# Column differences moved behind the last tile's second norm, and the first loads of down's weights moved behind the load for the fifth matrix

## The chip, the cores and the metric

The kernel runs on the 8 cores of one Trainium2 chip. Each core computes 1,024 of the 8,192 rows of the result: cores 2b and 2b+1 take the upper and the lower half of batch b. The cores share no data while they run. The time of a run is the device time of the slowest core, in microseconds (us).

## The reference, cut to what matters

The input x has shape (4, 2048, 2048). One layer of linear attention over the columns is followed by a gated feed-forward, each with a norm ahead of it and one behind it.

```python
X = Z_in[:, :256, :]; Y = Z_in[:, 256:, :]
att = relu((B_l @ X).T @ (C_l @ X))          # att[-1, -1] = 0
attn = concat(X + A_l @ (X @ att), Y + r_l * (Y @ att))

x = x + layernorm(attn(layernorm(x)))
# ffn(x), INTER = 5632, HIDDEN = 2048
g = (x @ gate_w.T) * gate_s
u = (x @ up_w.T) * up_s
out = ((silu(g) * u) @ down_w.T) * down_s
x = x + layernorm(ffn(layernorm(x)))
```

## The kernel before, in words

Everything is recorded in one list per engine (`Prog`), in the order of the calls in the source. An engine works its list strictly in that order, and a wait at the head of it holds everything behind it. GpSimd (POOL) has one list that holds nearly all loads of weights; SyncE (SP) has the loads and stores of x. POOL's DMAs also convert float32 in memory to bf16 on the core.

**First stage, attention and the two norms.** The 1,024 rows of a core are 8 tiles of 128, worked in the order `ORD` (index `i`, tile `dt = ORD[i]`; for `i` of 4 and more the two are the same). Tile `i` passes through `t0` (products with the attention matrix, L443), the first norm (`norm_a_...`, `x1`, L508, which also stores the tile by `spill[i]`), then the second norm: `square2` (ACT, L518: sum of squares into `q2a`), `norm_b_dv` (DVE, L525 to L531: three tiny operations, the last of which needs `q2a`), `norm_b_ac` (ACT L538 and L540, one tiny DVE operation L542, and ACT L545, which writes the normed tile `lc`). `ltr(i)` (L555) transposes `lc` on TensorE through two banks; ACT copies one out (L340), DVE the other (L341), both to `bop`. For tiles 4 to 7, three DVE subtractions (L570) then make the tile's columns of `T1`, `T2` and `T4`, operands of the second stage. They read both of the tile's copies.

**Second stage, gate and up.** The weights come as 44 packed matrices `m` (even: gate, odd: up; two of 5632/128 blocks each), 1 MB each on the core. `load_w(m)` puts matrix `m` into one of three buffers (`m % 3`). Matrices 0 and 1 are multiplied plainly (`plain_pe`, L732), first for the rows of half `h = 0` and then for `h = 1`. The matrices from 2 on go through seven products of 8 matmuls each in place of eight (Strassen-Winograd, `product(m, k)`, L799), for which `combos(m)` forms four sums of the matrix's quarters on DVE (L759). The loop over `m` issues products (m,6), (m,5), (m,7), (m+1,1), (m,4), (m+1,2), (m,3), and then `load_w(m + 3)`, which waits for product (m,3) to free the buffer. The first sum for matrix m+1 is recorded right behind product (m,6).

**Third stage, down, in blocks.** `down` (L837) multiplies the gated blocks `hdn` with down's weights `dwb`, of which `load_dw(gi)` loads block `gi` (0.5 MB on the core) into one of six buffers. The first `down` is recorded at m = 5, behind product (5,5). From then on it is woven into the loop over `m`.

**The stretch between the stages** is what the change touches. While tile 7 passes its norms, TensorE works plain products of the half h = 0, which need tiles 0 to 3 only: (0,0) and (1,0), then `ltr(6)`, then (0,1) and (1,1). Next comes `ltr(7)`, products (2,1) and (2,2), the four plain products of the half h = 1 (64 matmuls), and the loop. POOL's list there is: `load_w(2)`, the six `load_dw(0..5)`, `load_w(3)` (waits for `w_free[0]`, the last plain product with matrix 0), `load_w(4)` (waits for `w_free[1]`, the last one with matrix 1), `load_w(5)` (product (2,3)), `load_w(6)` (product (3,3)). `load_dw(gi)` waits for the stored and normed tile `i = 5 + gi // 2`, whose x buffer it overwrites.

Of the kernel before, what the change touches and what calls it, by code (L numbers as in the profile page):

```python
# [12 lines left out]
ALU = mybir.AluOpType  # L13
AX = mybir.AxisListType

P = 128
D = 2048
R = 1024
DT = R // P
# [9 lines left out]
ORD = [2, 3, 0, 1, 4, 5, 6, 7]  # L29
# [5 lines left out]
DS = 6  # L35
# [6 lines left out]
B11, B21, B12, B22, T1, T2, T4 = range(7)  # L42
# [69 lines left out]
def build_nc():  # L112
# [14 lines left out]
    pg = Prog(nc, es)  # L127
# [82 lines left out]
    def bank16(b):  # L210
        return ps[:, b, :].bitcast(BF16)
# [17 lines left out]
    x_ld, spill, lnf_done, x1_tok = {}, {}, {}, {}  # L229
# [108 lines left out]
    def evict(eng, out, in_, after):  # L338
        if eng == "scalar":
            return pg.ac(lambda e: e.copy(out, in_), after)  # L340
        return pg.dv(lambda e: e.tensor_copy(out, in_), after)  # L341
# [120 lines left out]
    sq1_t, va_t, ra_t, sqb_t, ltr_t, lnfT_t = {}, {}, {}, {}, {}, {}  # L462
    bop_t = {}
# [58 lines left out]
    def norm_b_dv(i):  # L522
        dt = ORD[i]
        c = slice(dt, dt + 1)
        a = pg.dv(lambda e: e.scalar_tensor_tensor(  # L525
            vb[:, c], s2a[:, c], -1.0 / (D * D), s2a[:, c],
            ALU.mult, ALU.mult), [x1_tok[i]])
        cn_t[i] = pg.dv(lambda e: e.scalar_tensor_tensor(
            cN[:, c], m1s[:, c], -1.0 / D, rN[:, c], ALU.mult, ALU.mult),
            [ra_t[i]])  # L530
        sqb_t[i] = pg.dv(lambda e: e.scalar_tensor_tensor(  # L531
            vb[:, c], q2a[:, c], 1.0 / D, vb[:, c], ALU.mult, ALU.add),
            [a, sqb_t[i]])

    def norm_b_ac(i):
        dt, sl = ORD[i], xslot[i]
        c = slice(dt, dt + 1)
        a = pg.ac(lambda e: e.activation(  # L538
            lnB[:, c], vb[:, c], AF.Ln, bias=eps_c[:, :]), [sqb_t[i]])
        a = pg.ac(lambda e: e.activation(  # L540
            r2[:, c], lnB[:, c], AF.Exp, scale=-0.5), [a])
        b = pg.dv(lambda e: e.scalar_tensor_tensor(  # L542
            ng2[:, c], s2a[:, c], -1.0 / D, r2[:, c], ALU.mult, ALU.mult),
            [a])
        lnf_done[i] = pg.ac(lambda e: e.activation(  # L545
            lc[:, i % 2, :], xr[:, sl, :], AF.Identity, scale=r2[:, c],
            bias=ng2[:, c]), [b])

    def ltr(i):
        dt = ORD[i]  # L550
        for g in range(2):
            bk = LNB[g]
            for k in range(8):
                ht = g * 8 + k
                t = pg.pe(lambda e, bk=bk, k=k, ht=ht: e.transpose(  # L555
                    bank16(bk)[:, k * P:(k + 1) * P],
                    lc[:, i % 2, ht * P:(ht + 1) * P], idm[:, 0, :]),
                    [lnf_done[i], *tok_bank[bk]] if k == 0 else (),
                    sig=(k == 7))
            o = (dt % 4) * P  # L560
            ev = evict(("scalar", "vector")[g],
                       bop[:, (B11, B21, B12, B22)[g + 2 * (dt // 4)], :,
                           o:o + P],
                       bank16(bk).rearrange("p (k c) -> p k c", c=P), [t])
            tok_bank[bk] = (ev,)
            lnfT_t.setdefault(dt // 4, {})[g] = ev
        if dt >= 4:
            for out, in0, in1 in ((T1, B12, B11), (T2, B22, T1), (T4, B21, T2)):
                bop_t[out] = pg.dv(lambda e, out=out, in0=in0, in1=in1:
                                   e.tensor_tensor(  # L570
                    bop[:, out, :, o:o + P], bop[:, in0, :, o:o + P],
                    bop[:, in1, :, o:o + P], ALU.subtract),
                    [*lnfT_t[0].values(), *lnfT_t[1].values(),
                     bop_t.get(in1)])
        ltr_t[i] = t


    w_ld, dw_ld, w_free = {}, {}, {}

    def load_w(m, after=()):  # L580

        s = m % WS
        w_ld[m] = pg.dma("gpsimd", f"w{s}", wr[:, s, 0:4, :],
                         t_gu.ap()[m], after)

    def dw_at(gi):
        return {IT - 2: dwx0, IT - 1: dwx1}.get(gi, dwb[:, gi % DS, :])

    def load_dw(gi, after=()):
        dw_ld[gi] = pg.dma("gpsimd", f"d{gi % DS}", dw_at(gi)[:, :],  # L590
                           t_dw.ap()[gi * P:(gi + 1) * P, :], after)
# [78 lines left out]
    for i in range(2, DT):  # L670
# [15 lines left out]
        t0(i, 0)  # L686
        t0(i, 1)
        ltr(i - 2)
        if nxt:
            prep_cast(i + 1, 0)  # L690
# [51 lines left out]
    def plain_post(m, gi, h, bk, t):  # L742
        f = gated if m else silu_of
        tok_bank[bk] = (f(gi, h, 2 + gi, ps[:, bk, :], [t]),)
# [46 lines left out]
    def product(m, k):  # L791
        a_bk = RING[2 * (m - 2) % 3]
        b_bk = RING[(2 * (m - 2) + 1) % 3]
        bk = {2: CB, 5: b_bk, 3: b_bk}.get(k, a_bk)
        ws, bs = PROD[k]
        need = [w_ld[m], *tok_bank[bk], cmb.get((m, ws)), bop_t.get(bs),
                *(lnfT_t[bs // 2].values() if bs < T1 and k != 7 else ())]
        for c in range(8):
            t = pg.pe(lambda e, c=c: e.matmul(  # L799
                ps[:, bk, :], wr[:, m % WS, ws, c * P:(c + 1) * P],  # L800
                bop[:, bs, c, :], start=(k in (1, 2, 5) and c == 0),
                stop=(c == 7), skip_group_check=(k not in (1, 2))),
                need if c == 0 else (), sig=(c == 7))
        if k == 1:
            copied(m, "P1", bk, t)
        elif k == 2:
            joined_up(m, "P1", bk, t, 0, 0)
        elif k == 6:
            copied(m, "U2", bk, t)
        elif k == 5:  # L810
            st[(m, "P5")] = t
            tok_bank[bk] = (t,)
        elif k == 7:
            copied(m, "U3", bk, t)
            joined_up(m, "U3", b_bk, st[(m, "P5")], 1, 1)
        elif k == 4:
            tok_bank[bk] = (used(m, 1, 0, ps[:, bk, :], t),)
        else:
            joined_up(m, "U2", bk, t, 0, 1)
            w_free[m] = t  # L820
# [49 lines left out]
    last = DT - 1  # L870
# [4 lines left out]
    x1(last)  # L875
    square2(last)
    ltr(last - 1)
    g1, u1 = plain_pe(0, 1, 0, 2), plain_pe(1, 1, 0, 3)
    norm_b_dv(last)
    norm_b_ac(last)  # L880
    plain_post(0, 0, 0, 0, g0)
    plain_post(1, 0, 0, 1, u0)
    plain_post(0, 1, 0, 2, g1)
    plain_post(1, 1, 0, 3, u1)
    ltr(last)
    tmp_free[0] = tmp_free[1] = (ltr_t[6],)
    tmp_free[2] = tmp_free[3] = (ltr_t[7],)
    product(2, 1)
    product(2, 2)
    for gi in range(DS):  # L890
        i = 5 + gi // 2
        load_dw(gi, [spill[i], lnf_done[i]])
    for n, (m, gi) in enumerate(((0, 0), (0, 1), (1, 0), (1, 1))):
        t = plain_pe(m, gi, 1, n)
        plain_post(m, gi, 1, n, t)
# [5 lines left out]
        bop[:, T3, :, :], bop[:, B22, :, :], bop[:, B12, :, :], ALU.subtract),  # L901
        [w_free[1], *lnfT_t[1].values()])
    load_w(4, [w_free[1]])

    for m in range(2, NM):
        b = next(k for k in range(NB) if 2 * (m // 2) < BASE[k] + BLKS[k])
# [26 lines left out]
        if b > 0 and n == 3:  # L933
            for li in range(BLKS[b - 1]):
                gi = BASE[b - 1] + li + DS
# [247 lines left out]
```

How the kernel before makes its waits and increments, by code:

```python
                def body(eng, ename=ename):  # L91
                    seen = {}
                    for after, fn, sem, n in self.lists[ename]:
                        for tok in after:
                            if tok is None:
                                continue
                            s, v = tok
                            if v > seen.get(s, 0):
                                eng.wait_ge(self.sems[s], v)
                                seen[s] = v
                        if fn is None:
                            continue
                        ins = fn(eng)
                        if sem is not None:
                            ins.then_inc(self.sems[sem], n)
```

## Time and profile before

| | |
|---|---|
| runs of the kernel (us) | 1055.66, 1155.41, 1055.39; median 1055.66 |
| profiled execution (us) | 1055.02 |
| its slowest core, core 7, from first to last instruction | 1053.5 |
| spans of cores 0 to 7 | 1050.1, 1052.8, 1052.2, 1050.6, 1049.5, 1051.4, 1050.7, 1053.5 |
| TensorE busy on core 7 | 1006.6 us, 96% of the span |
| VectorE busy | 591.6 us, 56% |
| ScalarE busy | 289.5 us, 27% |
| chain that ended last, by engine | PE 81%, DMA 5%, DVE 5%, ACT 5% |

The second run is a disturbed one, in which the whole chip is slower; it is left aside. Times in the rows are counted from the span's start. A row of the timeline is: start, length, engine, line, operation, what it writes and reads, count; the bracket behind it is the time that the engine sat idle before it, and what ended that. PE is TensorE, PEld its weight load, DVE VectorE, ACT ScalarE, POOL GpSimd. L86 is the helper that records every DMA.

### The profile page before, as it was taken

The page shows a single profiled execution, that of the slowest core. Times are in us where ns is not written, and L with a number is a line of the kernel's source. Part 1 is how long each engine was busy: PE and PEld are TensorE (multiplying, and loading weights), DVE is VectorE, ACT ScalarE, POOL GpSimd, SP SyncE. Part 2 cuts the span into 40 slices and gives each one's busy share as a digit, 9 for nine tenths or more (in the row PEclk, how much of TensorE's full clock was granted, in tenths as well). Part 3 has the DMA queues.
Part 4 walks back from the last instruction along what each step waited for, and adds up shares of the span by engine and source line. Part 5 has one row for each costly group of instructions (what it writes and reads, how often), then busy time and mean ns, then how long its engine had stood idle before and what let it go on. Part 6 is the DMA issues. An engine that isn't in the chain of part 4 may idle for free.

```text
span 1053.5 us, 12922 instructions; the slowest of 8 cores (1049.5 to 1053.5 us)
## 1 busy us (share of the span) xinstructions
PE 1006.6 (96%) x4868; PEld 461.8 (44%) x4868; DVE 591.6 (56%) x814; ACT 289.5 (27%) x427; POOL 52.1 (5%) x98
## 2 busy tenths in 40 slices
PE   2899999999999999999999999999999999999993
PEld 0345554444444444444444444444444444444441
DVE  3656667445646555654655555654555555555577
ACT  3555666622112012111112112111112121112266
POOL 0000000100001001001001001010010010001010
PEclk9999999999999999999999999999999999999997
DMA  7602331794234625626527329229238247338479
GB/s 210 144 1 110 113 138 50 149 162 81 46 69 79 116 52 87 114 41 104 97 40 123 77 40 147 54 40 159 41 53 147 40 73 128 49 71 162 119 120 200
DMA packets 18636, 101.35 MB, mean 96 GB/s; under 512 B 2192, under 2 KB 2320, under 8 KB 9744
## 3 DMA queue, kind: packets, MB, share of 16 engines
q0 software_dynamic: 13536, 75.50, 42.0%
q1 hardware_dynamic: 4608, 24.38, 6.5%
q10 hardware_dynamic: 432, 0.64, 0.3%
q8 instruction: 40, 0.66, 0.3%
q14 instruction: 20, 0.16, 0.1%
HBM read 152.95 MB, written 16.78 MB: 161 GB/s over the span
## 4 chain that ended last, share of the span: by engine, by line
PE 81%; DMA 5%; DVE 5%; ACT 5%; issue 3%; POOL 0%; DVEq 0%; ACTq 0%; SPq 0%; POOLq 0%
PE ps L799 45%; PE ps L837 28%; PE ps L443 4%; DMA dwb<-dw 3%; PE ps L412 2%; DMA wr<-gu 1%; DVE xr L508 1%; ACT lc L545 1%; DMA xr<-xtop 1%; ACT lc L468 1%; ACT pc L334 1%; PE ps L732 1%; ACT bop L340 1%; DVE acc L826 0%; DVE att L426 0%
## 5 line engine op out<-in xcount | busy, mean ns | idle before, releaser
L799 PE MATMUL ps<-bop,wr 128*128 128x512 bf16 x2352 | 520.0, 379 | 1.7 <-DMA wr<-gu 1.7
L799 PEld LDWEIGHTS ps<-bop,wr 128*128 128x128 bf16 x2352 | 229.9, 98 | 279.3 <-issue 2.5
L837 PE MATMUL ps<-dwb,hdn 128*128 128x512 bf16 x1344 | 307.2, 379 | 1.0 <-DMA dwb<-dw 0.9
L852 DVE TENSOR_TENSOR acc<-acc,ps 128x2048 f32<-128x2048 f32 x70 | 160.2, 2288 | 213.2 <-PE ps L837 213.2
L837 PEld LDWEIGHTS ps<-dwb,hdn 128*128 128x128 bf16 x1344 | 131.3, 98 | 160.5 <-issue 2.9
L772 ACT COPY tmp<-ps 128x512 f32<-128x512 f32 x126 | 73.3, 582 | 347.7 <-PE ps L799 347.7
L780 DVE TENSOR_TENSOR tmp<-tmp,ps 128x512 f32<-128x512 f32 x126 | 86.5, 686 | 92.1 <-ACT tmp L772 46.0
L759 DVE TENSOR_TENSOR wr<-wr 128x1024 bf16<-128x1024 bf16 x168 | 114.2, 686 | 8.2 <-DMA wr<-gu 3.7
L443 PE MATMUL ps<-att,xT 128*128 128x512 bf16 x512 | 117.4, 379 | 0.5 <-DVE xT L341 0.5
L710 ACT ACTIVATE sg<-tmp,cpks 128x512 bf16<-128x512 f32 x63 | 45.5, 722 | 239.7 <-DVE tmp L780 239.7
L443 PEld LDWEIGHTS ps<-att,xT 128*128 128x128 bf16 x512 | 49.5, 98 | 58.2 <-issue 1.0
L86 POOL DMA_DIRECT2D wr<-gu x44 | 23.5, 534 | 888.9 <-PE ps L799 625.6
L721 DVE SCALAR_TENSOR_TENSOR hdn<-tmp,cpks,sg 128x512 bf16<-128x512 f32 x63 | 47.3, 751 | 6.6
L412 PE MATMUL ps<-V,Xn 128*128 128x512 bf16 x128 | 36.2, 395 | 4.5 <-DVE att L426 1.9
L850 DVE COPY acc<-ps 128x2048 f32<-128x2048 f32 x8 | 18.3, 2292 | 25.4 <-PE ps L837 25.4
L721 DVE SCALAR_TENSOR_TENSOR hdn<-ps,cpks,sg 128x512 bf16<-128x512 f32 x25 | 18.6, 749 | 23.4 <-PE ps L799 11.1
L426 DVE TENSOR_SCALAR att<-ps 128x1024 bf16<-128x1024 f32 x16 | 19.6, 1225 | 19.8 <-PE ps L412 19.8
L710 ACT ACTIVATE sg<-ps,cpks 128x512 bf16<-128x512 f32 x25 | 17.1, 687 | 49.6 <-PE ps L799 46.5
L732 PE MATMUL ps<-bop,wr 128*128 128x512 bf16 x128 | 28.1, 379 | 0.0
L455 DVE SCALAR_TENSOR_TENSOR vp<-ps,sS,xr 128x512 f32<-128x512 f32 x32 | 23.3, 747 | 3.7 <-PE ps L443 3.7
L86 POOL DMA_DIRECT2D dwb<-dw x42 | 22.3, 550 | 17.1 <-ACT tmp L772 16.9
L981 ACT ACTIVATE junk<-acc 128x512 bf16<-128x512 f32 (+1 forms) x14 | 16.4, 1174 | 23.5 <-DVE acc L974 22.6
(93 smaller groups left out, 390.5 us busy)
## 6 DMA issues: line engine op xcount, KB each, us to landing
wr<-gu POOLq DMA_DIRECT2D x44, 1024.0 KB, 9.7
dwb<-dw POOLq DMA_DIRECT2D x42, 512.0 KB, 18.0
xr<-x SPq DMA_DIRECT2D x8, 1024.0 KB, 6.1
y<-xr SPq DMA_DIRECT2D x8, 1024.0 KB, 3.9
y<-acc POOLq DMA_DIRECT2D x6, 1024.0 KB, 8.8
x1r<-y SPq DMA_DIRECT2D x2, 1024.0 KB, 6.0
xr<-xtop SPq DMA_DIRECT2D x2, 512.0 KB, 9.1
xr<-xtop SPq DMA_DIRECT2D x4, 256.0 KB, 11.5
```

What stands on the lines that cost most here:

```text
L86: return self.put(eng, lambda e: e.dma_start(out, in_), after, sem, 16)
L412: t = pg.pe(lambda e, jt=jt: e.matmul(ps[:, bk, :], Xn[:, jt, nt * P:(nt + 1) * P], V[:, jt, q * MQ:(q + 1) * MQ], start=(jt == 0), stop=( ...
L443: t = pg.pe(lambda e: e.matmul(ps[:, bk, :], xT[:, i % 3, nt, :], att[:, nt, q * MQ:(q + 1) * MQ], start=(nt == 0), stop=(nt == NT - 1)), ...
L710: sl_t[q] = pg.ac(lambda e: e.activation(sg[:, q, :], src, AF.Silu, scale=cpk[:, C_GS + gi:C_GS + gi + 1]), [*after, *sg_free[q]])
L721: t = pg.dv(lambda e: e.scalar_tensor_tensor(hdn[:, gi % HS, h * MQ:(h + 1) * MQ], src, cpk[:, C_US + gi:C_US + gi + 1], sg[:, q, :], ALU. ...
L732: t = pg.pe(lambda e, ht=ht: e.matmul(ps[:, bk, :], wr[:, m, gi * 2 + ht // 8, (ht % 8) * P:(ht % 8 + 1) * P], bop[:, (B11, B21, B12, B22) ...
L759: cmb[(m, out)] = pg.dv(lambda e: e.tensor_tensor(u[:, out, :], u[:, in0, :], u[:, in1, :], op), [w_ld[m], *(cmb[(m, n)] for n in needs)])
L772: c = pg.ac(lambda e: e.copy(tmp[:, k, :], ps[:, bk, :]), [t, *tmp_free[k]])
L780: a = pg.dv(lambda e: e.tensor_tensor(tmp[:, k, :], tmp[:, k, :], ps[:, bk, :], ALU.add), [t, c])
L799: t = pg.pe(lambda e, c=c: e.matmul(ps[:, bk, :], wr[:, m % WS, ws, c * P:(c + 1) * P], bop[:, bs, c, :], start=(k in (1, 2, 5) and c == 0 ...
L837: t = pg.pe(lambda e, gi=gi, li=li, hc=hc: e.matmul(ps[:, banks[hc], :], hdn[:, gi % HS, tt * P:(tt + 1) * P], dw_at(gi)[:, hc * MQ:(hc + ...
L852: acc_t[tt] = pg.dv(lambda e: e.tensor_tensor(dst, dst, src, ALU.add), [t, acc_t[tt]])
```

## The change

The subtractions become a function of their own, `t_sums(i)`. For tiles 4 and 5 it is called where they stood. For tile 6 (`last - 1`) it is called behind `norm_b_dv(7)` and `norm_b_ac(7)`; for tile 7 it stays right behind `ltr(7)`. And the six `load_dw` calls move from behind `product(2, 2)` to behind `load_w(4, ...)`. Nothing is computed otherwise.

```diff
-        if dt >= 4:
-            for out, in0, in1 in ((T1, B12, B11), (T2, B22, T1), (T4, B21, T2)):
-                bop_t[out] = pg.dv(lambda e, out=out, in0=in0, in1=in1:
...
         ltr_t[i] = t
+        if dt >= 4 and i < DT - 2:
+            t_sums(i)
+
+    def t_sums(i):
+
+        dt = ORD[i]
+        o = (dt % 4) * P
+        for out, in0, in1 in ((T1, B12, B11), (T2, B22, T1), (T4, B21, T2)):
+            bop_t[out] = pg.dv(lambda e, out=out, in0=in0, in1=in1:
+                               e.tensor_tensor(
+                bop[:, out, :, o:o + P], bop[:, in0, :, o:o + P],
+                bop[:, in1, :, o:o + P], ALU.subtract),
+                [*lnfT_t[0].values(), *lnfT_t[1].values(),
+                 bop_t.get(in1)])
@@ -878,18 +884,17 @@
     g1, u1 = plain_pe(0, 1, 0, 2), plain_pe(1, 1, 0, 3)
     norm_b_dv(last)
     norm_b_ac(last)
+    t_sums(last - 1)
     plain_post(0, 0, 0, 0, g0)
...
     ltr(last)
+    t_sums(last)
     tmp_free[0] = tmp_free[1] = (ltr_t[6],)
     tmp_free[2] = tmp_free[3] = (ltr_t[7],)
     product(2, 1)
     product(2, 2)
-    for gi in range(DS):
-        i = 5 + gi // 2
-        load_dw(gi, [spill[i], lnf_done[i]])
     for n, (m, gi) in enumerate(((0, 0), (0, 1), (1, 0), (1, 1))):
...
     load_w(4, [w_free[1]])
+    for gi in range(DS):
+        i = 5 + gi // 2
+        load_dw(gi, [spill[i], lnf_done[i]])
```

On DVE, in the stretch between `x1(7)` (L508) and the copy of tile 7's transposes, the rows stand so before:

```order
185 L508 SCALAR_TENSOR_TENSOR xr,s2a<-vp,rN,xr 128x2048
186 L341 COPY bop<-ps 128x8x128
187 L570 TENSOR_TENSOR bop<-bop 128x8x128 x3
188 L525 SCALAR_TENSOR_TENSOR vb<-s2a 128x1
189 L528 SCALAR_TENSOR_TENSOR cN<-m1s,rN 128x1
190 L531 SCALAR_TENSOR_TENSOR vb<-q2a,vb 128x1
191 L542 SCALAR_TENSOR_TENSOR ng2<-s2a,r2 128x1
192 L721 SCALAR_TENSOR_TENSOR hdn<-ps,cpks,sg 128x512 x2
```

and so in the changed program (its line 577 is 570 of before, 727 is 721):

```order
185 L508 SCALAR_TENSOR_TENSOR xr,s2a<-vp,rN,xr 128x2048
186 L341 COPY bop<-ps 128x8x128
187 L525 SCALAR_TENSOR_TENSOR vb<-s2a 128x1
188 L528 SCALAR_TENSOR_TENSOR cN<-m1s,rN 128x1
189 L531 SCALAR_TENSOR_TENSOR vb<-q2a,vb 128x1
190 L542 SCALAR_TENSOR_TENSOR ng2<-s2a,r2 128x1
191 L577 TENSOR_TENSOR bop<-bop 128x8x128 x3
192 L727 SCALAR_TENSOR_TENSOR hdn<-ps,cpks,sg 128x512 x2
```

The three subtractions of tile 6 now stand behind all four of the norm's DVE operations for tile 7. On POOL, the head of the list of loads (`wr` is a matrix of gate or up, `dwb` a block of down's weights) changes so:

```order
-L86 DMA wr<-gu 128x4096 x3
+L86 DMA wr<-gu 128x4096 x5
 L86 DMA dwb<-dw 128x2048 x6
-L86 DMA wr<-gu 128x4096 x8
+L86 DMA wr<-gu 128x4096 x6
 L86 DMA dwb<-dw 128x2048 x4
 L86 DMA wr<-gu 128x4096 x4
```

The loads for matrices 3 and 4 now stand ahead of the six blocks, and the load for matrix 5 stands directly behind them. TensorE's and ACT's lists are the same in both programs, apart from line numbers.

## Rows read from the trace of the kernel before

**Rows 1.** Timeline of core 7, TensorE, between the stages:

```profile
207.25 1.05 PE L555 MATMUL ps<-idms,lc 128*128 128x128 bf16 x16 [1.66 <-ACT lc L545]
...
211.59 13.98 PE L732 MATMUL ps<-bop,wr 128*128 128x512 bf16 x64
225.41 5.34 PE L799 MATMUL ps<-bop,wr 128*128 128x512 bf16 x24
232.48 29.73 PE L799 MATMUL ps<-bop,wr 128*128 128x512 bf16 x137 [1.74 <-DMA wr<-gu]
```

**Rows 2.** The same timeline, VectorE:

```profile
201.35 2.29 DVE L570 TENSOR_TENSOR bop<-bop 128x1024 bf16<-128x1024 bf16 x3 [1.87 <-ACT bop L340]
...
203.81 0.16 DVE L531 SCALAR_TENSOR_TENSOR vb<-q2a,vb 128x1 f32<-128x1 f32 x1
204.76 0.16 DVE L542 SCALAR_TENSOR_TENSOR ng<-s2a,r 128x1 f32<-128x1 f32 x1 [0.79 <-ACT r L540]
...
210.54 0.68 DVE L341 COPY bop<-ps 128x1024 bf16<-128x1024 bf16 x1
...
232.44 1.49 DVE L759 TENSOR_TENSOR wr<-wr 128x1024 bf16<-128x1024 bf16 x2 [3.75 <-DMA wr<-gu]
...
253.21 1.48 DVE L759 TENSOR_TENSOR wr<-wr 128x1024 bf16<-128x1024 bf16 x2
```

**Rows 3.** The same timeline, ScalarE:

```profile
200.09 0.18 ACT L518 ACTIVATION_READ_ACCUMULATOR lc<-xr 128x1 f32 x1
200.19 0.99 ACT L340 COPY bop<-ps 128x1024 bf16<-128x1024 bf16 x1
...
205.01 2.09 ACT L545 ACTIVATE lc<-xr,ng,r 128x2048 bf16<-128x2048 f32 x1 [0.36 <-DVE ng L542]
```

**Rows 4.** The same timeline, GpSimd: issues of loads:

```profile
192.11 2.11 POOL L86 DMA_DIRECT2D dwb<-dw  x4
211.11 1.07 POOL L86 DMA_DIRECT2D dwb<-dw  x2 [16.88 <-ACT tmp L772]
219.21 0.54 POOL L86 DMA_DIRECT2D wr<-gu  x1 [7.04 <-PE ps L732]
226.12 0.53 POOL L86 DMA_DIRECT2D wr<-gu  x1 [6.37 <-PE ps L732]
240.10 0.53 POOL L86 DMA_DIRECT2D wr<-gu  x1 [13.45 <-PE ps L799]
```

**Rows 5.** Busy time by stretch, core 7: five engines, TensorE's clock, DMA share, GB/s:

```profile
196.00:226.00 30.00, 28.34 (x156) 13.63 (x154) 13.68 (x23) 11.53 (x14) 1.60 (x3) 1.00 1.02 173
```

**Rows 6.** Issues at 219.21 and at 240.10: count, size, us to landing:

```profile
wr<-gu POOLq DMA_DIRECT2D x1, 1024.0 KB, 13.1
...
wr<-gu POOLq DMA_DIRECT2D x1, 1024.0 KB, 8.6
```

**Rows 7.** Timeline of core 1, TensorE, at matrix 3:

```profile
232.13 30.12 PE L799 MATMUL ps<-bop,wr 128*128 128x512 bf16 x131 [2.65 <-DMA wr<-gu]
```

**Rows 8.** Timeline of core 5, TensorE, the same place:

```profile
225.08 37.29 PE L799 MATMUL ps<-bop,wr 128*128 128x512 bf16 x172
```

**Rows 9.** Chain that ended last, core 7: start, length, what:

```profile
232.48 34.69 PE ps L799 x160
```

**Rows 10.** Timeline of core 7, GpSimd: a later burst of loads:

```profile
328.16 0.53 POOL L86 DMA_DIRECT2D wr<-gu  x1 [18.47 <-PE ps L799]
328.68 2.12 POOL L86 DMA_DIRECT2D dwb<-dw  x4
340.25 0.53 POOL L86 DMA_DIRECT2D wr<-gu  x1 [9.45 <-PE ps L799]
```

**Rows 11.** First, fifth and sixth issue of that burst: us to landing:

```profile
wr<-gu POOLq DMA_DIRECT2D x1, 1024.0 KB, 9.9
...
dwb<-dw POOLq DMA_DIRECT2D x1, 512.0 KB, 21.5
...
wr<-gu POOLq DMA_DIRECT2D x1, 1024.0 KB, 16.7
```

More of the change, by code:

```diff
@@ L566, in ltr @@
             lnfT_t.setdefault(dt // 4, {})[g] = ev
-        if dt >= 4:
-            for out, in0, in1 in ((T1, B12, B11), (T2, B22, T1), (T4, B21, T2)):
-                bop_t[out] = pg.dv(lambda e, out=out, in0=in0, in1=in1:
[L570 to L574, printed above, removed]
-        ltr_t[i] = t
+        ltr_t[i] = t
+        if dt >= 4 and i < DT - 2:
[10 more added lines that the diff above has]
+                 bop_t.get(in1)])
     w_ld, dw_ld, w_free = {}, {}, {}
```

## The prediction

> **What bounds the kernel now.** The table of busy times comes first: TensorE works 96% of the span, so the time is TensorE's instructions plus the few gaps between them. The next view is therefore TensorE's timeline, searched for brackets with idle time, in the stretch that the change touches. It shows two gaps [rows 1]. Ahead of the last transposes (L555) TensorE sits idle 1.66 us, released by ACT's L545, which writes tile 7's normed rows. Ahead of product (3,1) it sits idle 1.74 us, released by the load of a matrix. Behind that one its row runs on without an idle bracket. After the gap work is dense, so whatever TensorE gains or loses here reaches the end unless a later wait takes it back.
>
> First gap. DVE's timeline has tile 6's three subtractions (L570, 2.29 us from 201.35) directly ahead of the norm's small operations, the last of which (L531) starts at 203.81 [rows 2]. What it needs, the sum of squares, is complete at 200.09 + 0.18 = 200.27 on ACT [rows 3]. The norm waits for DVE's list, and DVE in turn waited for ACT's copy (bracket of L570).
>
> Second gap. The load for matrix 3 is issued at 219.21 [rows 4] and takes 13.1 us to land, where the load for matrix 5, issued at 240.10, takes 8.6 [rows 6]. The table by stretches shows the DMA engines full (share 1.02) from 196 to 226 [rows 5]: the six blocks of down's weights, issued at 192.11 and 211.11, stand ahead of it [rows 4].
>
> **The subtractions.** The same three operations run, 2.29 us on DVE, only later. After the change L531 can start at about 200.4. ACT stands next: its copy L340 is ahead of the norm's logarithm in its list and ends at 200.19 + 0.99 = 201.18 [rows 3]. From L531's start to L545's start it is 205.01 - 203.81 = 1.20 us [rows 2, 3], so L545 starts by 201.18 + 1.20 = 202.4 and ends by 202.4 + 2.1 = 204.5. TensorE's plain products end at 207.25 - 1.66 = 205.59 [rows 1]. The norm is then 1.1 us ahead of TensorE, and the gap of 1.66 us goes in full, with no new gap in its place. The moved subtractions run from about 202.3 to 204.6, in time in which DVE has nothing (before, it is idle from 204.92 until ACT's first silu). What comes next on both engines (table load, silu, gating, the copies of tile 7) moves forward by some 2.6 us, while TensorE moves by 1.66; before, DVE's copy ends at 210.54 + 0.68 = 211.22, ahead of the plain products of h = 1 at 211.59 [rows 1, 2], so that wait does not open either. The other users of these differences stand behind 225 us. **Term: -1.66.**
>
> **Matrices 3 and 4.** Their loads wait for TensorE (`w_free[0]`, `w_free[1]`), and these points move by -1.66: issue at 217.55 and 224.46. Only matrix 2 and the store of tile 7 are ahead of matrix 3 now, both long landed, so 8.6 us [rows 6] give 226.2; with 1.3 us more for a load with another behind it (9.9 in place of 8.6, rows 6 and 11 compared [rows 6, 11]) 227.5. Product (3,1) wants it at 232.48 - 1.74 - 1.66 = 229.1. The gap of 1.74 us goes: **term -1.74** on this core. Matrix 4 lands at 224.46 + 9.9 = 234.4 and is wanted 7 products later, past 241. No wait.
>
> Not all cores had this gap: core 1 has 2.65 us [rows 7], core 5 none at all [rows 8]. The faster cores gain the 1.66 only.
>
> **The six blocks and matrix 5.** This is what I price highest. The six blocks (3 MB) are no longer spread over 192 to 226 but issued in one go behind matrix 4, at 225 to 228, and `load_w(5)` follows in the same list. Its own issue point moves from 240.10 to 240.10 - 3.40 = 236.7, by which time most of the six are still in the queues ahead of it. When does it land? A later burst is the same thing with four blocks: a matrix issued at 328.16, four blocks, a matrix issued at 340.25 [rows 10]. The first lands at 328.16 + 9.9 = 338.06; the last block, issued at 330.27, lands at 330.27 + 21.5 = 351.8; the second matrix at 340.25 + 16.7 = 356.95 [rows 10, 11]. So a block costs (351.8 - 338.06) / 4 = 3.43 us while the engines are full, and from the first issue to the last landing it is 28.8 us. With two more blocks: 28.8 + 2 x 3.43 = 35.7. Counted from matrix 4's issue at 224.46, matrix 5 lands at 260.1. In the burst nothing stood behind the second matrix; here matrix 6 is issued at about 249, which by the 1.3 us above would make it 261.4. I take the middle, 260.8, and 0.15 us until TensorE starts (landing at 232.3, start at 232.48).
>
> Who waits? Product (5,1) comes 14 products or 112 matmuls behind (3,1). A matmul in this run takes 34.69 / 160 = 0.217 us [rows 9], so before it is reached at 232.48 + 24.3 = 256.8, and after the change at 253.4. Before, DVE formed the first sums of matrix 5 at 253.21 without a wait, since it had landed at 240.10 + 8.6 = 248.7 [rows 2, 6]. After, DVE stops at these sums at about 250 and TensorE at 253.4, until 260.9: **term +7.5** (6.9 to 8.2 by the two ends).
>
> Behind the stopped DVE stand the join of product (4,7) and ACT's silu on it. They cost nothing more: the two first sums and the join take about 2.1 us, and TensorE has (5,1), (4,4) and (5,2) to do, 5.2 us, before (4,3) needs the join's bank. Before, matrix 3 showed the pattern: DVE idle 3.75, TensorE idle 1.74, then none [rows 1, 2]. Matrix 6 lands some 6 us behind matrix 5, at 267, and (6,1) comes 12.1 us behind (5,1), at 273: the queue has caught up. The blocks themselves have landed by 255 and the first `down` comes at about 268.
>
> **The sum.** On core 7: -1.66 - 1.74 + 7.5 = +4.1 us, from the profiled 1055.02 to 1059.1. On a core without the second gap it is +5.8; core 5 goes from 1051.4 to 1057.2, core 7 from 1053.5 to 1057.6, so core 7 still decides. The median of the runs shown is 0.6 us above the profiled one; I put the forecast between, at 1059.4.
>
> What speaks against this in the notes: the Trainium skill, "DMA: Bandwidth & Descriptors", section "Anatomy of one DMA — SWDGE (gpsimd) path", gives a DMA issued by GpSimd 2.0 us plus its bytes over 436 GB/s. With float32 as the bytes (10.5 MB for both matrices and six blocks), an estimate by that page is 26 us from matrix 4's issue, landing at 250.5, ahead of 253.4, and the sum would be -3.4. The trace does not agree: these loads move at 173 GB/s of bf16, or 346 GB/s of float32, with the engines full [rows 5].
>
> **The rivals.**
> *The queue drains in time (the other side).* If matrix 5 is there by 253.4, only the gains are left: 1055.0 - 3.4 = 1051.6 to 1052.3. For it speaks that a matrix behind the last block needed just 5.15 us for 1 MB (351.8 to 356.95), so the queue can be faster. Against it, the blocks are what fills it, at 3.43 us each. The result changes sign where matrix 5 lands at 256.8, for which the six blocks would have to take 4 us less, 2.8 each. 8%.
> *A partial wait.* Blocks at 2.8 to 3.1 us each, or a matrix 4 that lands early: a wait of 3.5 to 5.5 us, 1055 to 1057.2. 12%.
> *A deeper wait.* Up to seven loads are outstanding at once, where before the most seen is five [rows 10]. If GpSimd has to stop in the middle of the six until room is there, or all cores burst at once and share memory, matrix 5 lands at 263 to 266: 1061.5 to 1065. A stop alone costs nothing while the queues stay full, which is why I hold it low. 14%.
> *The change does less than it says.* The first gap stays, because ACT and not DVE holds the norm: then +5.8, about 1061. ACT's rows leave 1.1 us of room. 3%.
>
> **How the numbers follow.** The forecast, matrix 5 late by 6 to 9 us, has 63%. 2% of this kernel is 21 us, and about this much is what a measurement of it is taken to tell from no change; every case lies within, so "same" has nearly everything. The range leaves out the clean gain and the far end of the deeper wait: 1055.0 to 1062.5.
>
> **What would show it.** Right: no bracket ahead of L555; DVE's moved subtractions at about 202.3; no wait on a load at (3,1); then one bracket of 7 to 8 us ahead of (5,1), near 253 us, released by a load, beside a longer one on DVE's sums, and the load for matrix 5 with about 24 us to landing. Wrong: a load for matrix 5 that lands within 17 us, or a second wait on matrix 6 at 273, which would mean that the queue doesn't catch up and that the loss grows.

## The result, and the profile after

The changed kernel takes 1062.89 us (median; 1062.74 to 1064.44), the kernel before 1055.4 to 1057.4 beside it. The ratio is 1.0066, 95% interval 1.0054 to 1.0078: 5.7 to 8.2 us slower. The forecast was 1059.4, some 4 us slower, with a range up to 1062.5. The direction and the place were right, the size was too small, and the time lies above the range. Medians and ratios, here and below, are of the undisturbed executions alone; in the others the cores of one die, or of both, run at a lower granted clock.

| us | before | after |
|---|---|---|
| profiled execution | 1055.02 | 1062.74 |
| its slowest core | core 7, 1053.5 | core 3, 1061.2 |
| spans of cores 0 to 7 | 1050.1, 1052.8, 1052.2, 1050.6, 1049.5, 1051.4, 1050.7, 1053.5 | 1060.7, 1058.3, 1059.1, 1061.2, 1058.2, 1060.5, 1056.9, 1059.5 |
| mean of the eight spans | 1051.4 | 1059.3 |

From the page of the changed kernel: its span, TensorE's busy time, the slices with TensorE's granted clock and the DMA share, and two groups of instructions with the idle time before them. Line 805 is 799 of before, 765 is 759, 843 is 837.

```profile
span 1061.2 us, 12922 instructions; the slowest of 8 cores (1056.9 to 1061.2 us)
...
PE 1009.5 (95%) x4868; PEld 462.5 (44%) x4868; DVE 591.6 (56%) x814; ACT 289.6 (27%) x427; POOL 52.1 (5%) x98
...
PEclk9999999998999999999999999999999999999997
DMA  7603331379224734635626528329229237238479
...
L805 PE MATMUL ps<-bop,wr 128*128 128x512 bf16 x2352 | 522.8, 380 | 9.3 <-DMA wr<-gu 9.3
...
L765 DVE TENSOR_TENSOR wr<-wr 128x1024 bf16<-128x1024 bf16 x168 | 114.2, 686 | 17.7 <-DMA wr<-gu 13.2
```

TensorE has the same 4868 matmuls, yet it is busy 1009.5 us instead of 1006.6, and it waits 9.3 us for one load of a matrix, where before it waited 1.7. The clock's tenth slice, from 239 to 265 us, shows 8 where it showed 9 before. DVE waits 13.2 us for loads of matrices, before 3.7.

TensorE's timeline of core 3, from the end of the first stage to the first product with down's weights (L843). It answers [rows 1]:

```profile
204.52 1.06 PE L555 MATMUL ps<-idms,lc 128*128 128x128 bf16 x16
...
244.70 7.50 PE L805 MATMUL ps<-bop,wr 128*128 128x512 bf16 x34
261.46 13.32 PE L805 MATMUL ps<-bop,wr 128*128 128x512 bf16 x48 [9.26 <-DMA wr<-gu]
274.61 3.62 PE L843 MATMUL ps<-dwb,hdn 128*128 128x512 bf16 x16
```

The transposes at 204.52 have no bracket any more, and there is none at matrix 3. What is new is one gap of 9.26 us ahead of product (5,1) at 261.46, released by the load of matrix 5. All eight cores have it: 8.02, 7.49, 7.30, 9.26, 7.28, 8.57, 6.33 and 8.06 us, mean 7.8. The row behind it holds a second loss. Its 48 matmuls run from 261.46 to 274.61, 13.15 us. At the 0.216 us of full speed they would take 10.36.

VectorE on the same core, which answers [rows 2]: the norm's last operation ahead of the sum of squares' use (L531), L542, the moved subtractions (L577), and the first sums of matrices 3 and 5 (L765):

```profile
199.48 0.16 DVE L531 SCALAR_TENSOR_TENSOR vb<-q2a,vb 128x1 f32<-128x1 f32 x1 [0.77 <-ACT lc L518]
200.87 0.16 DVE L542 SCALAR_TENSOR_TENSOR ng<-s2a,r 128x1 f32<-128x1 f32 x1 [1.23 <-ACT r L540]
200.95 2.28 DVE L577 TENSOR_TENSOR bop<-bop 128x1024 bf16<-128x1024 bf16 x3
...
226.50 1.49 DVE L765 TENSOR_TENSOR wr<-wr 128x1024 bf16<-128x1024 bf16 x2 [0.53 <-DMA wr<-gu]
...
261.31 0.69 DVE L765 TENSOR_TENSOR wr<-wr 128x1024 bf16<-128x1024 bf16 x1 [12.64 <-DMA wr<-gu]
```

The norm no longer waits for the subtractions: L531 starts as soon as ACT's sum of squares is there, and they follow at 200.95. Matrix 5 holds DVE for 12.64 us.

GpSimd's issues on core 3 (loads of matrices 3 and 4, the six blocks, matrices 5 and 6), which answer [rows 4]:

```profile
216.48 0.53 POOL L86 DMA_DIRECT2D wr<-gu  x1 [25.31 <-PE ps L738]
223.39 0.53 POOL L86 DMA_DIRECT2D wr<-gu  x1 [6.38 <-PE ps L738]
223.94 3.17 POOL L86 DMA_DIRECT2D dwb<-dw  x6
235.47 0.53 POOL L86 DMA_DIRECT2D wr<-gu  x1 [8.37 <-PE ps L805]
247.56 0.53 POOL L86 DMA_DIRECT2D wr<-gu  x1 [11.55 <-PE ps L805]
```

And the time from issue to landing of the loads for matrices 3, 4 and 5, which answers [rows 6, 11]:

```profile
wr<-gu POOLq DMA_DIRECT2D x1, 1024.0 KB, 9.9
...
wr<-gu POOLq DMA_DIRECT2D x1, 1024.0 KB, 11.4
...
wr<-gu POOLq DMA_DIRECT2D x1, 1024.0 KB, 25.7
```

Matrix 3 lands at 216.48 + 9.9 = 226.4, in time (it took 13.1 us before). Matrix 4 lands at 234.8. Matrix 5, issued at 235.47, lands 25.7 us later at 261.2, that is 37.8 us after matrix 4's issue.

### The profile page after: what moved, and what is told of

It is laid out like the page before. It is cut to its first block, busy times and chain, and to the rows that moved or that the text cites. A ratio compares the mean times of both kernels' runs of the same rounds, so it can differ in the third digit from the quotient of the medians.

```text
span 1061.2 us, 12922 instructions; the slowest of 8 cores (1056.9 to 1061.2 us)
## 1 busy us (share of the span) xinstructions
PE 1009.5 (95%) x4868; PEld 462.5 (44%) x4868; DVE 591.6 (56%) x814; ACT 289.6 (27%) x427; POOL 52.1 (5%) x98
## 4 chain that ended last, share of the span: by engine, by line
PE 83%; DMA 7%; DVE 4%; ACT 4%; issue 2%; POOL 0%; DVEq 0%; ACTq 0%; SPq 0%; POOLq 0%
PE ps L805 44%; PE ps L843 27%; PE ps L443 5%; DMA dwb<-dw 3%; PE ps L738 3%; DMA wr<-gu 2%; PE ps L412 2%; DMA xr<-xtop 1%; DVE xr L508 1%; ACT pc L334 1%; ACT lc L545 1%; ACT lc L468 1%; DVE acc L832 0%; DVE att L426 0%; PE ps L394 0%
## 5 line engine op out<-in xcount | busy, mean ns | idle before, releaser
L805 PE MATMUL ps<-bop,wr 128*128 128x512 bf16 x2352 | 522.8, 380 | 9.3 <-DMA wr<-gu 9.3
L805 PEld LDWEIGHTS ps<-bop,wr 128*128 128x128 bf16 x2352 | 230.7, 98 | 288.9 <-issue 13.7
L843 PE MATMUL ps<-dwb,hdn 128*128 128x512 bf16 x1344 | 307.2, 379 | 1.1 <-DMA dwb<-dw 1.1
L843 PEld LDWEIGHTS ps<-dwb,hdn 128*128 128x128 bf16 x1344 | 131.2, 98 | 160.7 <-issue 3.6
L765 DVE TENSOR_TENSOR wr<-wr 128x1024 bf16<-128x1024 bf16 x168 | 114.2, 686 | 17.7 <-DMA wr<-gu 13.2
```

The lines of the kernel that those rows point to most:

```text
L765: cmb[(m, out)] = pg.dv(lambda e: e.tensor_tensor(u[:, out, :], u[:, in0, :], u[:, in1, :], op), [w_ld[m], *(cmb[(m, n)] for n in needs)])
L805: t = pg.pe(lambda e, c=c: e.matmul(ps[:, bk, :], wr[:, m % WS, ws, c * P:(c + 1) * P], bop[:, bs, c, :], start=(k in (1, 2, 5) and c == 0 ...
L843: t = pg.pe(lambda e, gi=gi, li=li, hc=hc: e.matmul(ps[:, banks[hc], :], hdn[:, gi % HS, tt * P:(tt + 1) * P], dw_at(gi)[:, hc * MQ:(hc + ...
```

## The experiments

The theory after the result has three terms: the sums save 1.66 us; the bunch of six blocks holds matrix 5 for 6 to 9 us; and TensorE's clock, which falls to half while TensorE idles in that gap and stays there for some us behind it, takes 1.5 to 2.8 us more. The rivals: the moved sums have a part in the loss; the lower clock is an effect that nobody pays for; the wait comes from GpSimd, which can only have so many loads outstanding, and not from the number of blocks ahead. Here is what the table by stretches shows of the clock on core 3. In each row the number behind the five engines is TensorE's granted clock, then the DMA share and GB/s:

```profile
core 3: us, PE busy (x) PEld busy (x) DVE busy (x) ACT busy (x) POOL busy (x), PEclk, DMA share, GB/s
...
252.00:254.00 2.00, 0.20 (x1) 0.00 (x0) 0.00 (x0) 0.59 (x1) 0.00 (x0) 1.00 1.21 197
254.00:256.00 2.00, 0.00 (x0) 0.00 (x0) 0.00 (x0) 0.00 (x0) 0.00 (x0) 1.00 1.03 172
256.00:258.00 2.00, 0.00 (x0) 0.00 (x0) 0.00 (x0) 0.00 (x0) 0.00 (x0) 0.73 1.01 156
258.00:260.00 2.00, 0.00 (x0) 0.00 (x0) 0.00 (x0) 0.00 (x0) 0.00 (x0) 0.50 1.04 160
...
264.00:266.00 2.00, 2.00 (x6) 0.73 (x5) 0.60 (x1) 0.80 (x2) 0.00 (x0) 0.50 0.53 111
266.00:268.00 2.00, 2.00 (x8) 0.82 (x7) 0.00 (x0) 0.03 (x1) 0.00 (x0) 0.71 0.02 4
268.00:270.00 2.00, 2.00 (x11) 0.91 (x10) 0.23 (x1) 0.66 (x1) 0.00 (x0) 1.00 0.00 0
```

TensorE's last matmul ahead of the gap ends at 252.2. The clock is 1.00 until 256, falls between 256 and 258, and is then 0.50 (1.2 in place of 2.4 GHz) for the rest of the gap and until TensorE, at work again from 261.46, has got to between 266 and 268. The Trainium skill, "TensorE: Matmul & The Clock Gate", section "Part 1: The HAM clock gate", says that the slow clock is what an idle TensorE gets and that activity releases it; the trace agrees.

**The sums alone.** The `load_dw` calls stand as in the kernel before, `t_sums` as in the changed one:

```diff
     product(2, 2)
+    for gi in range(DS):
+        i = 5 + gi // 2
+        load_dw(gi, [spill[i], lnf_done[i]])
...
     load_w(4, [w_free[1]])
-    for gi in range(DS):
-        i = 5 + gi // 2
-        load_dw(gi, [spill[i], lnf_done[i]])
```

> Tile 6's subtractions stand behind tile 7's norm as in the changed kernel; all loads stand as before. Theory (the sums alone save the 1.66 us ahead of the transposes, but matrix 3 is held by the full queues and not by its issue): no gap ahead of L555; the issue for matrix 3 moves to 217.5 but its landing stays near 232.3 on core 7's count, since the blocks ahead of it land at 226 in any case; so the gap at (3,1) grows by up to 1.66 where there was one. Net 0 to -0.5 us on the cores with that gap, -1.0 to -1.7 on those without, -0.5 us for the slowest core. Rival (each term stands alone): -1.7 us on every core. Rival (the moved sums cause part of the loss): slower than before by 1 us or more.

1054.27 us against 1053.94 of before, ratio 1.0005 (0.9996 to 1.0014): no gain, where 0.5 us was expected. No core has a gap ahead of L555. Four cores have one at (3,1) of 2.29 to 3.10 us (core 0 has 0.21) and spans of 1051.3 to 1052.7; the other four have spans of 1047.8 to 1048.9. One of the four, core 1, on TensorE:

```profile
231.20 36.05 PE L805 MATMUL ps<-bop,wr 128*128 128x512 bf16 x160 [2.77 <-DMA wr<-gu]
267.09 3.62 PE L843 MATMUL ps<-dwb,hdn 128*128 128x512 bf16 x16
```

The row holds more than the gap: 160 matmuls from 231.20 to 267.09 are 35.89 us, where 34.53 is full speed. On the four cores with the long gap these matmuls take 1.36 to 1.69 us too much, on the others nothing. The expectation had not priced that. The saved 1.66 us reaches the end where matrix 3 was in time anyway. The slowest core is one where it wasn't. There TensorE is ready earlier, but the matrix comes at about the same time (products (3,1) behind a gap start at 231.2 to 231.9 us, before at 229.4 to 232.5), so the gap grows (0.62 to 2.65 us before, 2.29 to 3.10 here), and with it comes the lower clock. So the moved sums pay only if matrix 3 comes in time.

**The loads alone.** Tile 6's subtractions ahead of the norm as before, the six loads moved:

```diff
     product(2, 2)
-    for gi in range(DS):
-        i = 5 + gi // 2
-        load_dw(gi, [spill[i], lnf_done[i]])
...
     load_w(4, [w_free[1]])
+    for gi in range(DS):
+        i = 5 + gi // 2
+        load_dw(gi, [spill[i], lnf_done[i]])
```

> The six blocks' loads stand behind the load for matrix 4 as in the changed kernel; the sums stand as before. Theory: the whole loss is here. A gap of 6.5 to 9.5 us ahead of (5,1), TensorE's granted clock at half before its end and for some us behind it (48 matmuls in 12 to 13.3 us instead of 10.4), the gap of 1.66 us ahead of L555 as before. 1.7 us slower than the changed kernel, so 8.0 to 9.0 us slower than before. Rival (the sums share in the loss): less than 6 us slower than before.

1062.47 us against 1053.94, ratio 1.0082 (1.0069 to 1.0095), 8.5 us slower. Gaps of 5.73 to 8.83 us, mean 7.3, the smallest below the 6.5 expected. Core 6, TensorE, both gaps:

```profile
206.92 1.05 PE L555 MATMUL ps<-idms,lc 128*128 128x128 bf16 x16 [1.67 <-ACT lc L545]
...
263.42 12.32 PE L799 MATMUL ps<-bop,wr 128*128 128x512 bf16 x47 [8.83 <-DMA wr<-gu]
```

The whole loss is here. The gap ahead of L555 is back, and the ratio is 0.0016 above the changed kernel's, about 1.7 us.

**The changed kernel again**, on the chip of the next three:

> The changed kernel itself, on the same chip as the next three, as their yardstick: 6.5 to 7.5 us slower than before; gaps of 6 to 9.5 us ahead of (5,1).

1061.96 us against 1055.01, ratio 1.0065 (1.0053 to 1.0078). Gaps of 6.41 to 8.49, mean 7.4; the 48 matmuls behind them take 1.3 to 2.9 us longer than at full speed, mean 1.9.

**The gap filled.** The changed kernel with 28 matmuls that nobody reads, where TensorE would idle:

```diff
         if m + 1 < NM:
+            if m == 4:
+                fill_bk = RING[2 * (m - 1) % 3]
+                for c in range(28):
+                    pg.pe(lambda e, c=c: e.matmul(
+                        ps[:, fill_bk, :], wr[:, 1, A22, 0:P],
+                        bop[:, B21, 0, :], start=True, stop=True),
+                        [*tok_bank[fill_bk]] if c == 0 else (), sig=False)
             product(m + 1, 1)
```

> The changed kernel with 28 extra matmuls (6.0 us at full speed) between products (4,7) and (5,1), on a bank that (5,1) clears; their results are not used and nothing is left out. They fill most of the gap. Theory (the idle time costs twice: the wait, and then TensorE at half its clock): granted clock 1.00 right through, the 48 matmuls behind the gap take 10.4 us instead of 12 to 13.2, so 1.5 to 2.8 us faster than the changed kernel although it does more. Rival (the wait alone costs, the lower clock is paid by nobody): same time as the changed kernel, within 0.7 us. Rival (the clock falls because of the load burst or the time, not because TensorE idles): clock at half all the same, no gain.

1059.72 us (ratio to the kernel before 1.0043, 1.0030 to 1.0057), 2.2 faster than the changed kernel's 1061.96 although it does more: 1058.67 to 1060.70 here, 1061.56 to 1062.68 there. In the profiled executions the mean of the eight spans falls from 1058.5 to 1056.4. On seven cores 0 to 1.7 us of gap are left, the clock stays at 1.00, and the 48 matmuls take 10.36 us. Core 2 (line 933 is the fill):

```profile
253.07 6.21 PE L933 MATMUL ps<-bop,wr 128*128 128x512 bf16 x28
260.80 10.52 PE L805 MATMUL ps<-bop,wr 128*128 128x512 bf16 x48 [1.52 <-DMA wr<-gu]
271.16 3.62 PE L843 MATMUL ps<-dwb,hdn 128*128 128x512 bf16 x16
```

On core 1 the load landed later, 3.59 us were left, the clock fell, and the 48 matmuls took 261.66 to 273.62, 11.96 us. It is this core that ended last (1059.1), and that execution took 1060.65, where two others took 1058.7 and 1058.8:

```profile
251.87 6.21 PE L933 MATMUL ps<-bop,wr 128*128 128x512 bf16 x28
261.66 12.12 PE L805 MATMUL ps<-bop,wr 128*128 128x512 bf16 x48 [3.59 <-DMA wr<-gu]
273.62 3.62 PE L843 MATMUL ps<-dwb,hdn 128*128 128x512 bf16 x16
```

So the lower clock is paid for, and it follows TensorE's idling: the burst of loads is the same on all eight cores, and the clock fell only on the one that idled longest.

**Five blocks ahead of matrix 5, then four.** The rest behind it (here for n = 5; n = 4 in the second):

```diff
     load_w(4, [w_free[1]])
-    for gi in range(DS):
+    for gi in range(0, 5):
         i = 5 + gi // 2
         load_dw(gi, [spill[i], lnf_done[i]])
...
                 load_w(m + 3, [w_free[m]])
+                if m == 2:
+                    for gi in range(5, DS):
+                        i = 5 + gi // 2
+                        load_dw(gi, [spill[i], lnf_done[i]])
```

> The changed kernel with the sixth block behind the load for matrix 5: five stand ahead of it. Theory (each block ahead of matrix 5 costs 3.4 us of its landing): gaps at (5,1) of 3 to 6 us, 3.4 less than with six; where they stay under about 4.5 us the clock keeps 1.00 and the saving is 3.4 plus the 1.5 to 2.8 of the clock. 4 to 6 us faster than the changed kernel. Rival (the wait is GpSimd running out of room for outstanding loads, so the number ahead matters little): 0 to 1.5 us faster.

1058.57 us against 1055.01, ratio 1.0032 (1.0020 to 1.0045), 3.4 us faster than the changed kernel. Gaps of 3.83 to 5.46 us, mean 4.7. The smallest is core 5's:

```profile
254.91 12.21 PE L805 MATMUL ps<-bop,wr 128*128 128x512 bf16 x48 [3.83 <-DMA wr<-gu]
266.95 3.62 PE L843 MATMUL ps<-dwb,hdn 128*128 128x512 bf16 x16
```

The expectation missed at the clock: I thought that gaps under about 4.5 us would leave it alone, which no run had shown, and the sums alone had already lost 1.4 to 1.7 us behind gaps of 2.3 to 3.1. They don't leave it alone. All eight cores lost 1.3 to 2.9 us behind the gap, mean 2.1, as many as with six blocks. So only the wait got shorter, and 4 to 6 us faster was too much.

> The same with four blocks ahead of matrix 5 and two behind it. Theory: gaps of 0 to 2.5 us, clock 1.00, 1.0 to 3.0 us faster than the kernel before and 8 to 9.5 us faster than the changed one. Rival (room for outstanding loads): gaps of over 4 us.

1053.78 us, ratio 0.9988 (0.9978 to 0.9997): faster than before by 1.2 us. Gaps of 0.38 to 2.33 us, mean 1.3, and none of the eight cores loses anything behind it. The largest:

```profile
253.99 10.52 PE L805 MATMUL ps<-bop,wr 128*128 128x512 bf16 x48 [2.33 <-DMA wr<-gu]
264.34 3.62 PE L843 MATMUL ps<-dwb,hdn 128*128 128x512 bf16 x16
```

48 matmuls, 253.99 to 264.34: 10.35 us. Mean gaps of 7.4, 4.7 and 1.3 us with six, five and four blocks ahead make 3.0 us for a block. The number of blocks ahead decides. That GpSimd had to stop for want of room is not seen in the changed kernel either: its six issues run on in 3.17 us, and the issue for matrix 5 waits for TensorE (`[8.37 <-PE ps L805]`).

**All six one place later**, behind the load for matrix 5:

```diff
     load_w(4, [w_free[1]])
-    for gi in range(DS):
-        i = 5 + gi // 2
-        load_dw(gi, [spill[i], lnf_done[i]])
...
                 load_w(m + 3, [w_free[m]])
+                if m == 2:
+                    for gi in range(0, DS):
+                        i = 5 + gi // 2
+                        load_dw(gi, [spill[i], lnf_done[i]])
```

> All six blocks in one bunch, one place later: behind the load for matrix 5 instead of 4. Theory (a bunch of six delays whichever matrix follows it; it has to go, not only to move): no wait at (5,1); matrix 6 lands near 273 (core 7's count) and is wanted at 269, since the first down adds 3.5 us ahead of it: gap of 3 to 6 us at (6,1), with TensorE's clock at half behind it for another 1 to 3; 2 to 5 us slower than before, 3 to 6 us faster than the changed kernel. Rival (matrix 5 is the only tight one): no gap, as fast as with the blocks dealt out.

1058.41 us against 1054.59, ratio 1.0037 (1.0023 to 1.0050). No gap at (5,1), but one of 2.16 to 4.92 us at (6,1), where 3 to 6 was expected. Core 4:

```profile
273.91 3.29 PE L805 MATMUL ps<-bop,wr 128*128 128x512 bf16 x8 [4.92 <-DMA wr<-gu]
277.60 3.61 PE L843 MATMUL ps<-dwb,hdn 128*128 128x512 bf16 x15 [0.40 <-DVE acc L856]
```

The 8 matmuls of (6,1) begin at 273.91, and the next product with down's weights comes 3.69 us later where 1.73 is full speed: 0.40 of it waits for DVE's copy of a down result, which stood behind the stopped sum of matrix 6, the rest is the clock at half. That wait on DVE I had not expected; it has up to 1.80 us (cores 1 and 5). At both places tried, a bunch of six delays the matrix that follows it.

**The blocks dealt out**, two each behind the loads for matrices 4, 5 and 6:

```diff
     load_w(4, [w_free[1]])
-    for gi in range(DS):
+    for gi in range(0, 2):
         i = 5 + gi // 2
         load_dw(gi, [spill[i], lnf_done[i]])
...
                 load_w(m + 3, [w_free[m]])
+                if m < 4:
+                    for gi in (2 * m - 2, 2 * m - 1):
+                        i = 5 + gi // 2
+                        load_dw(gi, [spill[i], lnf_done[i]])
```

> The sums as in the changed kernel; the six blocks are dealt out in pairs, behind the loads for matrices 4, 5 and 6. Theory (only the bunch ahead of matrix 5 costs): matrix 3 lands 9 to 10 us after its issue, matrix 5 near 248 (core 7's count), no wait on a load from 200 to 300 us, the clock stays at 1.00, both old gaps are gone: -1.66 us on cores without the second gap and -1.66 less that gap on the others; slowest core about -3, so 1052.5 to 1054. Rival (loads later than 225 us disturb the rest, or the first down waits for its blocks): a wait on dwb near 265, and no gain.

1051.13 us against 1053.94, ratio 0.9976 (0.9966 to 0.9986): 1.5 to 3.6 us faster than before, spans 1047.2 to 1049.5. On no core does TensorE wait for anything between 198 and 300 us. Matrices 3 and 5 on core 0, us from issue to landing:

```profile
wr<-gu POOLq DMA_DIRECT2D x1, 1024.0 KB, 9.5
...
wr<-gu POOLq DMA_DIRECT2D x1, 1024.0 KB, 12.7
```

**Only blocks 4 and 5 moved**, 0 to 3 loaded as before:

```diff
     product(2, 2)
+    for gi in range(0, 4):
+        i = 5 + gi // 2
+        load_dw(gi, [spill[i], lnf_done[i]])
...
     load_w(4, [w_free[1]])
-    for gi in range(DS):
+    for gi in range(4, 6):
```

> The sums as in the changed kernel; blocks 0 to 3 are loaded as before, at 192, in time when the queues have little else; only blocks 4 and 5 move behind the load for matrix 4. Theory: blocks 0 to 3 have landed at about 219, matrix 3 (issued 217.5) lands by 228, ahead of its need at 229; two blocks ahead of matrix 5 cost 6.9 us from 234, and it lands by 248 to 249, ahead of 253. No wait on a load, clock 1.00, same time as with the blocks dealt out: about -3 us on the slowest core. Rival (any block ahead of matrix 3 keeps it late): a gap of 1 to 2 us at (3,1) remains and the gain is 1.7 us less.

1051.35 us, ratio 0.9977 (0.9968 to 0.9985), the same as with the blocks dealt out, and again no core has a gap between 198 and 300 us. It was enough to take two of the six out of matrix 3's way.

**Dealt out, with and without the moved sums**, on one chip:

> The kernel with the blocks dealt out in pairs once more, as the yardstick for the next two on the same chip: 2 to 3.5 us faster than the kernel before, no wait on a load between 200 and 300 us.

> Blocks dealt out in pairs, but tile 6's subtractions back ahead of tile 7's norm. Theory: with no load late, the gap of 1.66 us ahead of L555 comes back and goes straight into the time: 1.3 to 2.0 us slower than with the sums moved, 0.5 to 1.5 us faster than before. Rival (what the sums save is lost again at the next point, as with the sums alone): same time as with the sums moved, within 0.4 us.

```diff
-        if dt >= 4 and i < DT - 2:
+        if dt >= 4 and i < DT - 1:
             t_sums(i)
...
-    t_sums(last - 1)
```

1052.25 us with them (ratio 0.9976, 0.9964 to 0.9987), 1054.05 without (0.9992, 0.9983 to 1.0002): 1.8 us, of which the gap that all eight cores have again is 1.7. Core 5:

```profile
207.10 1.05 PE L555 MATMUL ps<-idms,lc 128*128 128x128 bf16 x16 [1.68 <-ACT lc L545]
```

## Why the prediction was right in kind and too small in size

**The subtractions, -1.66: right.** The gap went in full, ACT was no obstacle (its copy ended and the norm ran on at once), and where no load is late the term is worth 1.7 us.

**Matrices 3 and 4, -1.74 on core 7: right for that core.** Matrix 3 landed 9.9 us after its issue on core 3 and 8.8 on core 7, within the 8.6 to 9.9 given, and no core waited for it.

**Matrix 5, +7.5: right in place and mechanism, nearly right in size.** On core 7, for which I counted, TensorE was ready at 253.4 as forecast, and matrix 5 landed at 261.2 (issue 236.71, 24.5 us to landing) where I had 260.8. Counted from matrix 4's issue I had it land after 36.3 us; on core 3 it was 37.8, of which 1.5 is matrix 4 itself (11.4 us to landing, not 9.9). The gap is 7.8 us on the mean of the cores, 7.3 and 7.4 in the two other runs. The four-block burst was the right row to scale [rows 10, 11], though the later runs put a block at 3.0 us and not at the 3.43 that I took from it. The estimate from the rate in the Trainium skill, "DMA: Bandwidth & Descriptors", section "Anatomy of one DMA — SWDGE (gpsimd) path", had matrix 5 landing 26 us after matrix 4's issue. The trace does not agree: it was 37.8 us on core 3.

**The step that failed: "They cost nothing more".** Behind the gap I looked for buffers and banks only, and for those the step holds: no bracket stands in the row from 261.46. But I took the gap of core 7 at matrix 3 for the pattern, 1.74 us and full speed behind it [rows 1], and so put TensorE's clock at nothing. What a longer gap costs more is TensorE's clock: 1.45 to 2.79 us on the eight cores, mean 2.1. And the kernel before had shown it, in a row that stands above [rows 7]. Core 1 had idled for 2.65 us, and its row has 131 matmuls in 30.12 us, where core 7's has 137 in 29.73. Here is core 1's timeline of before to the first product with down's weights, in a window of its own:

```profile
232.13 36.38 PE L799 MATMUL ps<-bop,wr 128*128 128x512 bf16 x160 [2.65 <-DMA wr<-gu]
268.35 3.62 PE L837 MATMUL ps<-dwb,hdn 128*128 128x512 bf16 x16
```

160 matmuls from 232.13 to 268.35 are 36.22 us, 1.69 more than the 34.53 of core 7. The table by stretches for the same core (five engines, then the granted clock) has the reason:

```profile
230.00:232.00 2.00, 0.00 (x0) 0.00 (x0) 0.00 (x0) 0.15 (x1) 0.00 (x0) 1.00 1.01 180
232.00:234.00 2.00, 1.87 (x5) 0.73 (x6) 1.81 (x3) 0.00 (x0) 0.00 (x0) 0.54 0.94 176
234.00:236.00 2.00, 2.00 (x7) 0.73 (x6) 1.38 (x3) 0.94 (x2) 0.00 (x0) 0.60 0.63 131
236.00:238.00 2.00, 2.00 (x11) 0.94 (x10) 0.00 (x0) 0.84 (x2) 0.00 (x0) 1.00 0.00 0
```

The clock is at about half for most of 232 to 236. The start of the kernel hints at the same for a longer idle time. On TensorE of core 7 of before, the same four matmuls of line 394 stand twice, 1.86 us behind 8.10 us of idling and 1.03 at work. The granted clock is recorded as 1.00 all through these first 40 us, so here the lengths alone say it:

```profile
18.95 1.86 PE L394 MATMUL ps<-Xn,gT 128*128 128x512 bf16 x4 [8.10 <-DVE Xn L279]
...
30.17 1.03 PE L394 MATMUL ps<-Xn,gT 128*128 128x512 bf16 x4
```

A forecast of a gap of 7 us had to put half the clock behind it.

**The second step: "core 7 still decides".** I credited the sum with core 7's own gap at matrix 3. After the change the cores are ordered by other things, their waits for matrix 5 above all (6.33 to 9.26 us), and the slowest one is core 3. It lost 1.65 (the same first gap) and 0.62 of old gaps, and gained one of 9.26 and 2.79 by the clock: +9.8 of the 10.6 us between its spans, 1050.6 and 1061.2. The remaining 0.8 is in its first 20 us, where the first product of the scores starts 0.83 later (20.85 instead of 20.02 us). In the other three executions the slowest core is 2, 4 and 4, so that it is core 3 here is chance.

The sums close. Core 7's own is -3.4 + 8.06 + 1.45 = +6.1, measured +6.0. On the mean of all cores, the old gaps at matrix 3 weigh 0.84 and core 1's clock behind one of them 0.21: -1.66 - 0.84 - 0.21 + 7.79 + 2.14 = +7.2, measured +7.9. The profiled execution lies 3.6 us above my 1059.1: about 1.4 by the clock on core 7, 0.5 by its longer gap, and 1.7 because core 3 ends that much behind core 7. With the clock's 2.1 alone my terms would have put core 7 at 1059.7 (it ended at 1059.5) and core 5 at 1059.3 (1060.5, since its gap was 8.57 and not 7.5).

Of the rivals, the queue did not drain in time, and the deeper wait is not what happened: the latest landing was 261.9 us, on core 5, where that rival had 263 to 266. The stop of GpSimd for lack of room is not seen: the six issues took 3.17 us, as each took 0.53 before. That the queue catches up by matrix 6 was right; no run of the changed kernel has a wait there.

**Better than both:** the sums moved, and the blocks dealt out in pairs or only two of them moved. They are 2.3 to 2.8 us faster than the kernel before in three comparisons (0.9976, 0.9977, 0.9976).

## What to carry to other kernels

A load that is moved out of one tight load's way is moved into the way of the next one: list every load behind the new place with its landing and the moment at which it is wanted, and deal a bunch out between them. Price a long gap of TensorE with what comes behind it, too, since its clock may be at half when the data are there. And on eight cores don't take it that the core that was slowest stays so: the new wait differed by 2.9 us between the cores, and the time is that of the core where start, old gaps and new wait add up to most.

## What the runs showed of the hardware

How long TensorE may idle before its clock falls can't be told from a gap's length. Behind 18 gaps of 0.21 to 2.33 us at matrices 3 and 5 all matmuls up to the first `down` ran at full speed. Behind 38 gaps of 2.29 to 9.26 us at the same places 1.3 to 2.9 us were lost, each time. The loss did not follow the gap's length: 2.94 us behind 5.04, and 1.45 behind 8.06. At matrix 6 the clock fell also behind a gap of 2.16 us, shorter than one that left it alone (core 7 of the run with the bunch one place later). The gap ends at 268.85, and the clock is down from about 270, ahead of the next gap, 1.02 us that end at 272.53:

```profile
268.00:270.00 2.00, 1.16 (x5) 0.51 (x6) 1.20 (x2) 0.00 (x0) 0.00 (x0) 0.95 1.06 176
270.00:272.00 2.00, 1.51 (x4) 0.30 (x2) 2.00 (x2) 0.40 (x1) 0.00 (x0) 0.50 1.02 164
```

Which core waits for its matrix changes. With the sums alone it was cores 1, 2, 4 and 6 that waited over 2 us, one of each two neighbours (0 and 1, 2 and 3, and so on), while the other had next to nothing; before, those with a wait of any length were 1, 2, 3 and 7. With the bunch one place later one of each two waits 0.9 to 2.4 us longer than the other. Why one of two gets its matrix later was not tried, and so it stays open whether the cores' bursts slow each other.
